# Values of eight heads by seven products of halves, in blocks 2 and 3 of a gated cross-attention block

## The reference

```python
x = x + tanh(g_xattn) * xattn(layernorm(x), ctx, mask, pair_bias, Wq, Wk, Wv, Wo)
x = x + tanh(g_ffn) * ffn(layernorm(x), weight, bias, lora_A, lora_B, lora_start_indices)
# xattn: x, ctx [32, 64, 512]; Wq, Wk, Wv [512, 32*128]; Wo [32*128, 512]
q, k, v = hidden_q @ Wq, hidden_kv @ Wk, hidden_kv @ Wv          # 32 heads of 128
score = einsum('bqhd,bkhd->bhqk', q, k) * scale + position_bias  # 64 x 64 per batch, head
probs = softmax(where(mask, score, -inf)), masked rows 0
return einsum('bhqk,bkhd->bqhd', probs, v).reshape(b, lq, h * dh) @ Wo
# ffn: y = x @ weight.T + bias + (lora, rank 16, by batch)
```

## Time and profile before

| what | before |
|---|---|
| median of 3 runs | 1740.77 us (1740.27 to 1741.35) |
| the profiled execution, whole | 1740.83 us |
| its span in the trace | 1739.0 us |
| TensorE busy | 1721.0 us, 99% |
| VectorE, ScalarE, GpSimd busy | 66%, 40%, 46% |
| DMA | 194 GB/s on average |

### The profile page before, as it was taken

How to read it: one execution, slowest core, us unless ns; L and a number is a source line. 1 busy time by engine, 2 the same in 40 slices (tenths; PEclk the granted TensorE clock), 3 DMA queues, 4 the chain that set the end, 5 groups by cost and what they waited for, 6 DMA issues and landing times.

```text
span 1739.0 us, 25524 instructions
## 1 busy us (share of the span) xinstructions
PE 1721.0 (99%) x8634; PEld 1460.0 (84%) x8634; DVE 1153.3 (66%) x2521; ACT 696.6 (40%) x1481; POOL 792.9 (46%) x1067
## 2 busy tenths in 40 slices
PE   8999999999999999999999999999999999999998
PEld 7788888888888888888888888888888888888887
DVE  5677667777676665666666666566666766666664
ACT  5555555554333442343333343233433333333331
POOL 5667766775344432344344343334443443333431
PEclk9999999999999999999999999999999999999999
DMA  7777777766445444545445454355454454454431
GB/s 277 267 261 264 269 269 267 281 248 218 180 170 200 170 169 157 189 176 196 167 168 195 167 190 177 135 201 192 164 182 181 170 188 170 160 191 164 171 127 55
DMA packets 111524, 336.63 MB, mean 194 GB/s; under 512 B 13377, under 2 KB 13505, under 8 KB 111394
## 3 DMA queue, kind: packets, MB, share of 16 engines
q1 hardware_dynamic: 111250, 334.73, 54.5%
q10 hardware_dynamic: 144, 0.26, 0.1%
HBM read 263.64 MB, written 71.30 MB: 193 GB/s over the span
## 4 chain that ended last, share of the span: by engine, by line
PE 94%; DVE 2%; issue 1%; DMA 1%; ACT 1%; POOL 1%; SPq 0%; ACTq 0%; DVEq 0%
PE vo_bank L309 13%; PE vo_bank L311 13%; PE vo_bank L310 13%; PE q_bank L309 7%; PE q_bank L311 7%; PE q_bank L310 7%; PE k_bank L309 6%; PE k_bank L311 6%; PE k_bank L310 6%; PE pv_two L314 5%; PE s_two L314 5%; PE s_two L315 2%; PE pv_two L315 2%; PE vo_bank L590 1%; DVE score L950 0%
## 5 line engine op out<-in xcount | busy, mean ns | idle before, releaser
L1197 POOL TENSOR_TENSOR score<-score,row_max 128x256 f32<-128x256 f32 x128 | 78.9, 616 | 683.7 <-DVE row_max L955 683.6
L1132 POOL TENSOR_TENSOR ot_lo<-attn,ot_hi 128x512 fp32r<-128x512 f32 x128 | 166.1, 1298 | 149.0 <-ACT ot_hi L696 149.0
L309 PE MATMUL q_bank<-xt_hi,wq 128*128 128x512 f32 x512 | 208.6, 407 | 0.0
L768 ACT ACTIVATE attn<-pv_two 128x512 f32<-128x512 f32 x128 | 76.7, 599 | 316.9 <-PE pv_two L315 316.9
L311 PE MATMUL q_bank<-xt_hi,wq 128*128 128x512 f32 x512 | 200.7, 392 | 0.0
L310 PE MATMUL q_bank<-xt_lo,wq 128*128 128x512 f32 x512 | 200.1, 391 | 0.0
L309 PE MATMUL k_bank<-ct_hi,wk 128*128 128x512 f32 x512 | 199.5, 390 | 0.2 <-DVE ct_lo L888 0.2
L950 DVE SCALAR_TENSOR_TENSOR score<-s_two,raw_bias 64x256 f32<-64x256 f32 x256 | 107.8, 421 | 138.2 <-PE s_two L315 135.9
L310 PE MATMUL k_bank<-ct_lo,wk 128*128 128x512 f32 x512 | 199.4, 389 | 0.0
L311 PE MATMUL k_bank<-ct_hi,wk 128*128 128x512 f32 x512 | 199.3, 389 | 0.0
L309 PE MATMUL vo_bank<-wv,ct_hi 128*128 128x512 f32 x504 | 196.2, 389 | 0.0
(11 more groups left out here) (196 smaller groups left out, 3835.2 us busy)
## 6 DMA issues: line engine op xcount, KB each, us to landing
wv<-wv_split SPq DMA_DIRECT2D x96, 512.0 KB, 5.3
wq<-wq_split SPq DMA_DIRECT2D x96, 512.0 KB, 3.2
wk<-wk_split SPq DMA_DIRECT2D x96, 512.0 KB, 3.6
wo<-wo_split SPq DMA_DIRECT2D x96, 512.0 KB, 5.2
raw_bias<-in_pair_bias SPq DMA_DIRECT2D x64, 256.0 KB, 5.8
wq_split<-wq SPq DMA_DIRECT2D x32, 512.0 KB, 2.9
wk_split<-wk SPq DMA_DIRECT2D x32, 512.0 KB, 4.1
wv_split<-wv SPq DMA_DIRECT2D x32, 512.0 KB, 5.9
```

The costliest lines, as they stand in the source:

```text
L309: pe.matmul(to, left[0], right[0], start=first, stop=False)
L768: act.activation(by(attn, PB), pv_two[:, :, 1, :], ACT.Copy).then_inc(ot_b, 1)
L1132: pool.tensor_tensor(to, src, f32(of), ALU.subtract).then_inc(done, 1)
L1197: pool.tensor_tensor(score[:, :, :], score[:, :, :], row_max[:, :].unsqueeze(2).to_broadcast([P, PB, S]), ALU.subtract).then_inc(shift_don ...
```

## The change

From group 16 on (the first of block 2), two groups, called a **pair** u (groups 2u and 2u+1, u = 8 to 15), are computed together. Their values are [512 x 512] @ [512 x 1024]; each operand is cut in four quarters, and seven products of sums of quarters take the place of eight. A product is two tiles of 6 matmuls, so a pair has 84 in place of 96.

- Products are done in the order 1, 2, 6, 7, 4, 5, 3, in the slots that held values: 1 and 2 in slot 8u-5, 6 and 7 in 8u-4, 4 alone in 8u-1, 5 and 3 in 8u. At the start of a block (u = 8 and 12) the first two slots are 8u-3 and 8u-2, which also hold `output` and `turn`. The first product of a slot stands ahead of its scores, the second behind them.
- No slot but these has values work of blocks 2 and 3: slots 91, 92, 123 and 124, in which values were computed before, have none.
- ACT copies product 1 to `values`; DVE adds each other one to a running sum (one addition a tile, two for product 5) before the bank is free.
- POOL makes the sums of weights and context in 20 **rounds** of four additions and two subtractions: weights in the odd slots 33 to 51 and 61 to 71, context in 54, 58, 86 and 90. SP writes them to device memory (`wv_mixed`, `ctxt_mixed`), and reads them back for the products. ACT makes their high parts.
- The context pieces move to s = 21, 22, 25 and 26. The probabilities overwrite `score`, and `prob` is gone.

```diff
-X_LOAD, LEAD_SUMS, LEAD_PIECES, LEAD_TURNS = 21, (22, 25), (23, 24, 27, 28), (25, 26, 29, 30)
+X_LOAD, LEAD_SUMS, LEAD_PIECES, LEAD_TURNS = 21, (22, 25), (21, 22, 25, 26), (25, 26, 29, 30)
+LEAD_CHUNKS = (0, 2, 1, 3)
...
+T_ROUNDS = [*range(33, 52, 2), *range(61, 72, 2)]
+S_ROUNDS = [H * b + s for b in (1, 2) for s in (22, 26)]
...
+def products_at(n):
+    for u in range(FIRST_PAIR, PAIRS):
+        first = 2 * G * u - (3 if u % 4 == 0 else 5)
+        slots = (first, first + 1, 2 * G * u - 1, 2 * G * u)
+        if n in slots:
+            return u, ((1, 2), (6, 7), (4,), (5, 3))[slots.index(n)]
...
-    if n % G == G - 1 and n < LAST:
+    if n % G == G - 1 and n // G + 1 < 2 * FIRST_PAIR:
         return n // G + 1, (0, 1)
...
+            def product(u, p, t):          # TensorE
+                job, number = ("w", u, p, t), product_number(u, p)
+                if t == 0:
+                    pe.wait_ge(product_in[number % 2], 16 * (number // 2 + 1))
...
+                emptied(pe, USED_LAST[job])
+                for k in range(2):
...
+                    mm = mm3(pe, bank_of(job)[:, :], left, parts(v_w, slice(None), 2 * (number % 2) + k, slice(None)),
+                             k == 0, k == 1)
+                mm.then_inc(vo_ps, 1)
...
                 if dense_at(n):
                     dense(*dense_at(n))
+                products(n, 0)
                 scores(n)
+                products(n, 1)
                 attention(n - 1)
...
+            def products(n, k):            # VectorE
+                u, found = products_at(n)
+                fourth, second, third, top = (2 * u + 1, 1), (2 * u + 1, 0), (2 * u, 1), (2 * u, 0)
+                for p in found[k:k + 1]:
+                    steps, after = {1: ((), None), 2: (((fourth, top),), 1), 6: (((fourth, second),), 1),
+                                    7: (((second, fourth),), 6), 4: (((fourth, third),), 7),
+                                    5: (((fourth, fourth), (second, second)), 4), 3: (((second, second),), 5)}[p]
+                    for t in range(2):
+                        if steps:
+                            dve.wait_ge(vo_ps, NUMBER["w", u, p, t] + 1)
+                            emptied(dve, ("w", u, after, t))
+                        for of, to in steps:
+                            if p in (2, 6, 4):
+                                dve.wait_ge(v_lo, V_READ[to])
+                            last = dve.tensor_tensor(values_f[:, v_block(*to), t, :], bank_of(("w", u, p, t))[:, :],
+                                                     values_f[:, v_block(*of), t, :], ALU.add)
+                        if steps:
+                            last.then_inc(vo_free, 1)
...
+            def mix(n):                    # GpSimd, last in slot n
...
+                for z, (to, left, right, op) in enumerate(steps):
+                    if z > 0:
+                        pool.wait_ge(mix_done, 4 * r + z)
+                    pool.tensor_tensor(to, left, right, op).then_inc(mix_done, 1)
```

More of the change, by code:

```diff
@@ L132, in jobs_in @@
         found += [("dense", *dense_at(n))]
+    if products_at(n):
+        u, products = products_at(n)
+        found += [("w", u, p, t) for p in products for t in range(2)]
     return found
@@ L161 @@
 V_BLOCKS = 6
+V_PLACE = {(g, half): (2 * g + half) % V_BLOCKS for g in range(2 * FIRST_PAIR) for half in range(2)}
+V_READ = {}
+_read = {place: G * g + G for (g, half), place in V_PLACE.items()}
+for _u in range(FIRST_PAIR, PAIRS):
+    for _l, _half in ((1, 1), (0, 0), (1, 0), (0, 1)):
+        _place = min(_read, key=_read.get)
+        V_PLACE[2 * _u + _l, _half], V_READ[2 * _u + _l, _half] = _place, _read[_place]
+        _read[_place] = G * (2 * _u + _l) + G
 def v_block(g, half):
-    return (2 * g + half) % V_BLOCKS
+    return V_PLACE[g, half]
 def raw_count(n):
@@ L271, in flamingo_block @@
             sem(f"{m}_done") for m in ("score_b", "score", "max", "shift", "sum", "inv", "rscale", "prob"))
+        product_in, sums_in, weights_in = ([sem(f"{m}_in{i}") for i in range(2)] for m in ("product", "sums", "weights"))
+        mix_done, mix_hi, mix_lo, mix_hi_saved, mix_lo_saved = (
+            sem(f"mix_{m}") for m in ("done", "hi", "lo", "hi_saved", "lo_saved"))
         stats_done, aggr_done, rstd_done, xn_done = (
@@ L303, in bank_of, with mixed, halves @@
             return banks[PLACE[job]]
+        def mixed(what):
+            return raw_vo if what == "weights" else stage
+        def halves(t):
+            return t[:, 0:HALF], t[:, HALF:2 * HALF]
         def k_part(part):
@@ L461, in _ @@
                     piece(3)
-                elif at:
+                elif at and not (at[1] == "context" and b > 0):
                     piece(at[0] + 2)
@@ L471, in _ @@
                         load(acc[(b + 1) % 2][:, t, :], x[PB * (b + 1) + t], x_in[t])
+                if round_at(n - 1):
+                    save_mixed(n - 1, 0)
+                if n == H:
+                    load_weights(0)
+                if round_at(n - 2):
+                    r, what, i = round_at(n - 2)
+                    if what == "weights" and i + 1 < len(T_ROUNDS):
+                        load_weights(i + 1)
+                    elif what == "context":
+                        mix_saved(r)
+                        piece(8 * (i // 2 + 1) + 6 + 2 * (i % 2))
+                        piece(8 * (i // 2 + 1) + 7 + 2 * (i % 2))
+                product_loads(n)
             pair_back(SLOTS)
@@ L753, in main_job, with products, mixed_part @@
                     values(g, tiles[k])
+            def products(n):
+                if products_at(n) and products_at(n)[1][0] == 1:
+                    u = products_at(n)[0]
+                    g, half = 2 * u + 1, 1
+                    for t in range(2):
+                        act.wait_ge(v_lo, V_READ[g, half])
+                        act.wait_ge(vo_ps, NUMBER["w", u, 1, t] + 1)
+                        act.activation(values_f[:, v_block(g, half), t, :], bank_of(("w", u, 1, t))[:, :],
+                                       ACT.Copy).then_inc(v_free, 1)
+            def mixed_part(n, k):
+                r, what, i = round_at(n)
+                act.wait_ge(mix_done, 4 * (r + 1))
+                wait(act, mix_hi_saved, 16 * (2 * r + k))
+                wait(act, mix_lo, 2 * r + k)
+                hi(mixed_hi[:, :], mixed(what)[k][:, :], mix_hi)
             def probabilities(n):
@@ L776, in exps @@
             def exps(n):
-                wait(act, turn_done, n)
                 act.wait_ge(shift_done, n + 1)
-                hi(prob[:, :, :], score[:, :, :], exp_done, ACT.Exp)
+                hi(score[:, :, :], score[:, :, :], exp_done, ACT.Exp)
             def turn(norm, b, t):
```

181 lines of the change are left out of this document (162 added, 19 removed).

## The result

| what | before | after |
|---|---|---|
| median of the runs | 1740.87 us (1740.27 to 1741.35) | 1779.76 us (1774.44 to 1783.33, four runs) |
| ratio after / before | | 1.0221 (1.0195 to 1.0247) |
| the profiled execution, whole; its span | 1740.83; 1739.0 | 1779.24; 1777.4 |
| mean granted clock of the four runs | 0.998 (profiled) | 0.990 (profiled), 0.992, 0.988, 0.986 |

Slower by 38.9 us, where 16.6 was forecast; 1779.76 lies above the range. The direction was right, the size was not. The page, against the earlier trace rows: matmuls 96 fewer, VectorE busy 70.4 us longer, GpSimd 105.1.

The account below looks back on a forecast made before the run. TensorE's own issue was taken to bound the kernel, with a 10.0 us chain per slot as floor. New waits of 38.4 us less 21.8 of matmuls gave +16.6 on 1740.77: 1757.4 us, range 1747 to 1769.

Parts of the forecast that it names:

- a slot has a floor of 10.0 us: Every slot: the chain from its scores over VectorE to `kt` starts anew, so none is shorter than 10.0 us.
- the term came to 9.7 of 11.6: Empty slots 91, 92, 123, 124: waits of 2.69 us each ahead of scores, plus 0.8 for `v_lo`; 11.6 us.
- 11.8 + 4.0 + 7.2 + 2.2: Waits in slots 8u-1 and 8u: ordinary 11.8, u = 8, 12 4.0, u = 10, 14 7.2; output bank (61, 62, 93, 94) 2.2.
- Rival (a): VectorE's idle time covers its additions, only the empty slots lose: 1730.6 us, faster; 10%.
- GpSimd's rounds at nothing in full slots: Full slots with a round: additions bring `v_lo` to T+11.7, with 1.1 us to the attention; no cost.
- the term for slot 91: Slot 91: `v_lo` comes behind a round's four additions on GpSimd, and the attention of 90 waits; +0.8 us.
- likeliest case has none or one: TensorE's clock: at most one fall to half clock in the likeliest case, which had 55%.
- rival (c): TensorE's clock falls behind the four 2.7 us waits: 1762.4 us with two falls, 1767 with four; two or more 22%.
- transfers at nothing: Loads of the products' weights and sums: each has a slot or more until wanted, so no waits were priced.
- rival (b): Transfers late in slots 8u-5 and 8u-4: if 2 us a pair stick, 16 us more, 1773 us; 8%.
- The prediction's own sign of being wrong: Wrong if TensorE waits for loads of `wv`, slots 8u take 12.8 us, or full slots with a round exceed 12.76.
- 8432 matmuls: A sign that would show the forecast right: TensorE has 8432 matmuls in the changed program.

Follow-up runs that it names:

- e1_empty: The kernel before, less 72 values matmuls, all taken from slots 91, 92, 123 and 124: 1732.36 us.
- e4_late: The changed kernel, with VectorE's two additions of product 4 behind its row sums, not ahead of its score instructions: 1773.70 us.
- e11_best: The changed kernel with late additions where n mod 4 = 3, products reordered and spread, earlier loads, earlier `lora_u`, rounds behind the next `v_lo`: 1749.60 us.
- e3_bytes: The changed kernel, with loads of the products' weights and sums cut to 8 of 128 partitions, all instructions and waits kept: 1767.54 us.
- e6_pre: The changed kernel, with the loads of sums for products 6 and 7 asked for one slot earlier: 1770.01 us.
- e5_spread: The changed kernel, with products of pairs 11 and 15 spread over six slots, so slots 91, 92, 123 and 124 hold 12 matmuls each: 1765.99 us.
- e9_nomix: The changed kernel, with the rounds' additions and subtractions on GpSimd cut to 8 columns: 1774.84 us.
- e7_fill: The changed kernel, with nine unneeded matmuls between keys and scores in each of slots 91, 92, 123 and 124: 1774.30 us.

## Why the prediction was wrong in size

- **TensorE's order sets the time, and a slot has a floor of 10.0 us.** Right. The scores of slot 123 came 9.95 us behind those of 122; e1_empty shows the floor on the kernel before, and the term came to 9.7 of 11.6. In slots 91, 92 and 124 the distances were 10.28, 12.66 and 10.79, as 92 and 124 had half clock in them and 92 the wait for `v_lo`. Slots 92 and 124 waited 1.7 us and not 2.69, because their queries ran at half clock (1250.72 to 1257.55 and 1680.80 to 1684.20) and so filled a part of the wait; the difference stands in the clock's row.
- **VectorE's additions cost 11.8 + 4.0 + 7.2 + 2.2.** Right in place and near in size: 9.1, 1.4, 7.5 and 2.6. Rival (a), that idle time covers them, is refuted by the waits in slots 8u; e4_late shows the queue to be the cause, as only the place of two additions changes there and the waits of slots 72, 104 and 120 are gone from its trace. e11_best, which changes several things, has 4.6 us less of `lora_u`.
- **GpSimd's rounds at nothing in full slots.** Right: in slots 33 to 51 and 54 the eleven rounds cost nothing that the trace shows. In blocks 2 and 3 they had 2.0 us of waits for `v_lo`, the term for slot 91 among them; slot 87's 1.5 us was not named.
- **The failed step: "likeliest case has none or one" fall of the clock.** Seven came from slot 68 on, 13.9 us by the account, less what slots 1 and 2 lost more in the kernel before: 12.9. The step took from the earlier trace rows that a wait of 1.84 us is harmless, and priced rival (c) by the four waits of 2.7 us alone. That was one execution. The same wait in slot 1, 1.82 to 1.84 us, stands in all fourteen traces of this case, and in ten of them, the changed kernel's included, the clock fell within 2.1 us behind it. The falls at 984.49, 1428.22 and 1523.79 came behind waits of 1.3 to 1.8 us, with one of 0.52 us just ahead of the first two, and that at 926.46 in a wait for weights. The price of one was near, 1.5 to 2.9 us against 2.5; their number was wrong. The Trainium skill (TensorE: Matmul & The Clock Gate, section "HAM oscillation — how this bites in real kernels") tells of a kernel in which bursts of matmuls are parted by DMA waits of some 3 to 5 us, and each burst begins throttled; the trace agrees for the 3.62 us in slot 68, and its falls behind 1.3 to 1.8 us go beyond that.
- **The second failed step: transfers at nothing**, with 8% for rival (b). They cost 10.5 us of waits, against the 16 that (b) named. The argument "each load has a slot or more until it is wanted" overlooked that it then takes 8.2 us in the median where before took 5.3 for half the bytes, and that four are asked for at once. e3_bytes gained 12.2 and e6_pre 9.8, both clear of noise. The prediction's own sign of being wrong, loads of `wv` that TensorE waits for, came.
- **The sum.** Forecast +16.6: waits 38.4, no clock, no transfers. The engines' waits were 31.9 and the transfers 10.5, so the waits' total of 42.4 was near for the wrong reason, and by luck: the engines' terms were 6.5 too high. The miss of 21.8 us in the profiled execution is the clock 12.9, the transfers 10.5, small delays 4.1 and 0.8 in slots up to 60, less those 6.5. The sign "8432 matmuls" was miscounted: 8634 of the earlier trace rows less 96 is 8538, which the trace has.

What stays open: why such a wait is followed by a fall in one execution and not in another. The runs of the changed kernel, 1774.44 to 1783.33 us, order themselves as their granted clocks do (0.992, 0.990, 0.988 and 0.986 from the fastest on), and e5_spread's one run of 1776.5 has the lowest clock of its four (0.986). An estimate from these: 0.006 less of mean clock is 21 us more at half clock, up to 10.7 us of issue, and the runs lie 8.9 apart. How many falls there were in a run without a trace wasn't seen.

## What to carry to other kernels

Fewer matmuls help only in slots that stay above the floor of the chain that starts anew in each; take the same saving evenly (14.5 of 16.3 us) and not in heaps (8.6). When work moves to another engine, look up its place in that engine's queue and what is behind it, since its busy share (69% here) didn't tell it. Price a new wait of TensorE at its length and again at what half clock behind it may cost (some 1.6 us a fall here), do not take one execution without a fall as proof that there is none, and look at how many loads a slot asks for at once, beside how many bytes.

## What the runs showed of the hardware

- The granted clock fell to 0.50 for 3.41 us behind waits of 1.29 us (984.49 and 1428.22), though it stayed at 1.00 behind the same wait at 1641.94. Behind one and the same wait of 1.82 to 1.84 us in slot 1 it fell in ten of fourteen traces. Falls were 3.41 or 6.83 us long.
- 3.41 us at half clock cost 1.65 us in slots 118 to 123 (e9_nomix 62.26 us, the changed kernel 60.61, with the same waits).
- 36 matmuls of 8.2 us, put where TensorE waited, made these slots 0.9 us shorter (e7_fill).
- In stretch 926.46 to 933.29 the core moved 414 GB/s, over the 358 of the earlier trace rows, while TensorE waited for weights.
- Between a wait's idle time as shown and the delay of the next start lie 0.16 us (0.389 shown for a matmul, 0.227 from start to start), so thirty waits cost some 5 us more than the list of waits adds up to.
